# Grouped-query layer: mask addition and segment maximum in one VectorE instruction per 128 columns

## The reference

```python
scores = jnp.einsum('bkgld,bksd->bkgls', q, k) * scale
scores = scores + encoder_attention_mask[:, :, None, :, :]
attn = jax.nn.softmax(scores, axis=-1)
out = jnp.einsum('bkgls,bksd->bkgld', attn, v)
out = out.transpose(0, 3, 1, 2, 4).reshape(b, l, H)
out = out @ Wo + bo
x = out + hidden_state
mu = jnp.mean(x, axis=-1, keepdims=True)
var = jnp.var(x, axis=-1, keepdims=True)
return (x - mu) * jax.lax.rsqrt(var + EPS) * gamma + beta
```

## Time and profile before

| | |
|---|---|
| median of 3 runs | 2688.79 us (2685.13 to 2689.0) |
| profiled execution, its time | 2687.89 us |
| its span, first to last instruction | 2686.1 us |
| busy in the span: PE | 2477.0 us (92%) |
| DVE, ACT, POOL | 1280.0 (48%), 1089.2 (41%), 1106.1 us (41%) |
| layer 1 stands at | about 805 to 1190 us of the span |

### The profile page before, as it was taken

How to read it: one execution, slowest core, us unless ns; L and a number is a source line. 1 busy time by engine, 2 the same in 40 slices (tenths; PEclk the granted TensorE clock), 3 DMA queues, 4 the chain that set the end, 5 groups by cost and what they waited for, 6 DMA issues and landing times.

```text
span 2686.1 us, 47930 instructions
## 1 busy us (share of the span) xinstructions
PE 2477.0 (92%) x18464; PEld 2080.4 (77%) x18464; DVE 1280.0 (48%) x2527; ACT 1089.2 (41%) x3705; POOL 1106.1 (41%) x1972
## 2 busy tenths in 40 slices
PE   7999998999997788758889899999899999899999
PEld 5887886888886666647778788888788888688887
DVE  4555564323226878764555533322355555432322
ACT  4555553111117777754565511111355555311111
POOL 2454446400035888873454571003335444640000
PEclk9999999999998989878999999999999999999999
DMA  4112213111122222221232241102211211311100
GB/s 154 56 56 74 86 48 95 59 47 48 57 71 72 82 91 70 74 67 45 94 111 77 82 129 48 47 23 69 87 48 49 84 53 48 95 59 48 47 32 16
DMA packets 110320, 181.25 MB, mean 67 GB/s; under 512 B 7888, under 2 KB 43408, under 8 KB 109072
## 3 DMA queue, kind: packets, MB, share of 16 engines
q1 hardware_dynamic: 110096, 178.19, 20.2%
HBM read 132.02 MB, written 46.14 MB: 66 GB/s over the span
## 4 chain that ended last, share of the span: by engine, by line
PE 79%; DVE 8%; ACT 6%; POOL 3%; issue 3%; DMA 1%; SPq 0%; DVEq 0%; POOLq 0%; ACTq 0%
PE banks L317 70%; PE banks L453 4%; ACT plain_high L697 4%; PE banks L480 3%; DVE neg_max L948 2%; DVE plain_high L944 2%; POOL plain_high L1268 1%; DVE plain_work L953 1%; PE banks L504 1%; DVE rounded_work L1046 1%; DVE rounded_work L1020 1%; DVE stats L1072 1%; POOL rounded_high L308 0%; PE banks L442 0%; ACT plain_high L684 0%
## 5 line engine op out<-in xcount | busy, mean ns | idle before, releaser
L317 PE MATMUL banks<-rounded_work,rounded_low 128*128 128x512 f32 (+1 forms) x2688 | 534.7, 357 | 58.4 <-issue 35.2
L1268 POOL TENSOR_SCALAR plain_high<-plain_high,inv_sum 128x128 f32<-128x128 f32 (+1 forms) x1024 | 389.6, 403 | 410.2 <-DVE inv_sum L966 409.7
L317 PEld LDWEIGHTS banks<-rounded_work,rounded_low 128*128 128x128 f32 x2688 | 446.7, 200 | 125.6 <-issue 53.7
L317 PE MATMUL banks<-rounded_work,rounded_high 128*128 128x512 f32 (+1 forms) x2400 | 485.4, 356 | 8.4 <-DMA rounded_work<-ctx_split 5.8
L925 ACT ACTIVATE plain_work<-banks,columns 128x512 f32<-128x512 f32 x192 | 132.5, 690 | 865.3 <-PE banks L317 865.3
L317 PEld LDWEIGHTS banks<-rounded_work,rounded_high 128*128 128x128 f32 x2400 | 397.1, 191 | 75.8 <-issue 10.0
L1244 DVE CAST rounded_work<-plain_work 128x512 fp32r<-128x512 f32 x192 | 99.3, 517 | 694.1 <-ACT plain_work L925 682.9
L317 PE MATMUL banks<-rounded_low,rounded_work 128*128 128x512 f32 x1728 | 413.1, 391 | 0.0
L317 PE MATMUL banks<-rounded_high,rounded_work 128*128 128x512 f32 (+1 forms) x1728 | 392.7, 380 | 0.0
L317 PEld LDWEIGHTS banks<-rounded_low,rounded_work 128*128 128x128 f32 x1728 | 322.3, 188 | 68.8 <-issue 3.0
L317 PEld LDWEIGHTS banks<-rounded_high,rounded_work 128*128 128x128 f32 x1728 | 311.8, 190 | 60.4 <-issue 1.4
(11 more groups left out here) (101 smaller groups left out, 3055.3 us busy)
## 6 DMA issues: line engine op xcount, KB each, us to landing
plain_work<-x SPq DMA_DIRECT2D x96, 256.0 KB, 2.8
plain_work<-mlp_w SPq DMA_DIRECT2D x96, 256.0 KB, 2.7
rounded_work<-ctx_split SPq DMA_DIRECT2D x24, 1024.0 KB, 5.9
u<-plain_work SPq DMA_DIRECT2D x48, 256.0 KB, 3.1
plain_work<-u SPq DMA_DIRECT2D x12, 1024.0 KB, 7.2
x<-plain_work SPq DMA_DIRECT2D x48, 256.0 KB, 2.1
plain_work<-attention_w SPq DMA_DIRECT2D x44, 256.0 KB, 2.7
plain_work<-inputs_t SPq DMA_DIRECT2D x8, 1024.0 KB, 8.0
```

What stands on the lines that cost most here:

```text
L317: mm = pe.matmul(dst, lhs(i), rhs(j), start=first and n == 0, stop=last and n == 2, skip_group_check=True)
L1268: last = pool.tensor_scalar(part, part, inv_sum[:, R % 2, r, g:g + 1], 1.0, ALU.mult, ALU.mult)
```

## The change

The two VectorE instructions of a bank give way to four of a fused kind, one for each segment. `tensor_tensor_reduce` with these operands writes out = (score + mask) * -1 and gives accum = min(3e38, all of out), which is the negated maximum. The SBUF copy therefore holds negated masked scores, and ScalarE's exp takes scale -1 in this layer. The wait between the addition and the reduction, on VectorE itself, goes. `s_free[r]` is now counted after the last of the four instead of after the addition, `maxed` isn't counted in this layer, and ScalarE waits for `s_free[r]` in its place; the later layers' counts of `maxed` are moved accordingly.

```diff
         def act_exp(act, y, p, k, r):
             R = y.round(p, k)
             pr = prob(y)[R % 2]
-            act.wait_ge(maxed, 4 * R + r + 1)
+            if y.kind == GQA:
+                act.wait_ge(s_free[r], y.use(p, k) + 1)
+            else:
+                act.wait_ge(maxed, 4 * (R if y.n == 0 else R - L[1].rounds) + r + 1)
             for g in range(y.segs):
                 part = slice(g * y.seg, (g + 1) * y.seg)
-                src = pr[:, r, part] if y.kind == GQA else PS[:, r, part]
-                last = act.activation(pr[:, r, part], src, ACT.Exp, bias=neg_max[:, R % 2, r, g:g + 1],
+                gqa = y.kind == GQA
+                last = act.activation(pr[:, r, part], pr[:, r, part] if gqa else PS[:, r, part], ACT.Exp, scale=-1.0 if gqa else 1.0,
+                                      bias=neg_max[:, R % 2, r, g:g + 1],
                                       accum_out=row_sum[:, R % 2, r, g:g + 1])
             last.then_inc(exped if y.kind == GQA else s_free[r], 1)
...
                 b = of_round(y, k)[0]
                 if k == 0 and r == 0:
                     dve.wait_ge(qk_loaded[p % 2], 16 * (p // 2 + 1))
-                dve.tensor_tensor(pr[:, r, :].rearrange("p (u n) -> p u n", u=4), src.rearrange("p (u n) -> p u n", u=4),
-                                  qk_mask[:, p % 2, b, :].unsqueeze(1).broadcast_to([P, 4, P]), ALU.add).then_inc(s_free[r], 1)
-                dve.wait_ge(s_free[r], u + 1)
-                src = pr[:, r, :]
+                for g in range(4):
+                    part = slice(g * P, (g + 1) * P)
+                    last = dve.tensor_tensor_reduce(pr[:, r, part], src[:, part], qk_mask[:, p % 2, b, :], -1.0, 3.0e38, ALU.add, ALU.min,
+                                                    accum_out=neg_max[:, R % 2, r, g:g + 1])
+                last.then_inc(s_free[r], 1)
+                return
             dve.tensor_reduce(neg_max[:, R % 2, r, 0:y.segs], src.rearrange("p (g n) -> p g n", g=y.segs), AX.X, ALU.max,
                               negate=True).then_inc(maxed, 1)
```

## The result

The changed kernel takes 2673.35 us in the median of 4 runs (2672.15 to 2673.65), the kernel before 2688.89 us (4 runs, 2685.13 to 2691.57): the ratio is 0.994, with a 95% interval of 0.9928 to 0.9952. It is 15.5 us or 0.6% faster. The forecast was 2678 us, with a range that began at 2673: the direction and the place are as foretold, the size is half as large again, and the median lies 0.35 us inside the lower end.

The account below looks back on a forecast made before the run. Layer 1 was taken as bound by hand-overs between four engines, mainly VectorE and ScalarE: 58 banks x 0.20 us = 11.6, less 1, leaves -10.5; 2687.9 - 10.5 + 0.9 = 2678 us, range 2673 to 2727.

Parts of the forecast that it names:

- the later release: TensorE may rewrite a bank some 0.4 us later; claimed to cost nothing, covered by 4.9 us, else 13 us in all.
- The fused instruction: Four per bank on VectorE in layer 1, each 0.28 us alone and taking the engine for 0.21 us.
- The dearer row, with a scalar column: Upper bound for the fused instruction: the nearest VectorE row of that width, 342 ns alone, taking the engine 0.26 us.
- the wash: Rival: fused instruction 0.26 us plus write 0.07, a bank 1.32 us as before, no change, 2689 us; chance 0.17.
- The accumulator write: One after each fused instruction on VectorE: 0.07 us of the engine, no hold, making a segment 0.28 us.
- Held reads: Rival: VectorE's accumulator writes and fused instructions never overlap, a bank 1.72 us, 37 us slower, 2726 us; chance 0.23.
- The banks on the chain: Layer 1 banks whose saving counts: 58 of 128, between 61 from chain shares and 56 from 7 a pair.
- The cut for the other branch: 1 us taken from the 11.6 us gain for rounds where GpSimd's normalisation, with 0.25 us of wait, ends last.
- the rival that takes the gain: GpSimd's normalisations, 311 us of 385 busy, end last in layer 1: only -5.5 us, 2683 us; chance 0.07.
- All other stretches as long as before: Sign in the profile: the layer 1 window shorter by 10 us, everything outside it unchanged.
- 1.1 us from a bank's first start to the next bank's: Sign in the changed kernel's profile: the length of a layer 1 bank on VectorE, against 1.32 us before.
- The inversions' wait for exp: Sign on VectorE in layer 1: the wait for ScalarE should stay at 1.6 us or grow.

Follow-up runs that it names:

- e2: The changed kernel with an unread maximum over 392 columns ahead of each bank's fused instructions, so a bank takes 1.32 us again; 2687.8 us, ratio 1.0003 to the kernel before.
- e9: The changed kernel with an unread maximum over 280 columns ahead of each bank's fused instructions, bank 1.19 us; 2680.66 us, ratio 0.9978 to the kernel before.
- e3: The kernel before with its addition and reduction, but each bank released and handed to ScalarE by one count after the reduction; 2687.09 us, ratio 1.0001.
- e4: The changed kernel with bank 0 of each layer 1 round normalised on VectorE instead of GpSimd; 2664.45 us, ratio 0.9915 to the kernel before.
- e8: The kernel before with bank 0 of each layer 1 round normalised on VectorE instead of GpSimd; 2688.27 us, ratio 1.0005.

## Why the prediction was right and wrong

- **Place, sign, mechanism.** Right in these: the gain is the shorter bank on VectorE (e2, e9), in layer 1, and nothing came of the dropped wait, of ScalarE's constant, or of the later release (e3).
- **The fused instruction.** Right: 0.28 us alone and 0.21 us to the next start, from the addition's row and the row with constant scalars. The dearer row, with a scalar column, would have been wrong; so the wash falls.
- **The accumulator write.** Wrong: "I take 0.07 us and no hold". It has no hold, but it takes nothing at all of the engine. This made a bank 1.12 us instead of 0.84, and the saving of a bank 0.20 instead of 0.48. It is the step of the prediction that failed: the term was taken from one-column instructions that stand alone and from ScalarE's read the earlier trace rows, and neither behaves like this write. Held reads, the case for slower, are refuted by the same rows: the write starts 0.08 us before its fused instruction ends (908.79, and 908.59 + 0.284).
- **The banks on the chain.** Too few: "I use 58", from a pattern of 7 a pair. The slope between 1.32 and 1.07 us is (385.8 - 370.4) / 0.25 = 62 banks by the stretches and 71 by the ratios (17.7 us), against the 61 that the shares of the chain had given and the 64 of the chain by GpSimd. Rounding the measured share down to the pattern cost 7% or more.
- **The cut for the other branch.** Wrong in size: "I take 1 us". At the bank of 0.84 us the slope would give 0.48 x 62 = 30 us. The layer 1 stretch gave 19.9 and the kernel 15.5. GpSimd's list, which now waits once a pair, was named as the rival that takes the gain, with 0.25 us of slack read rightly; but it was priced against the small saving and given 0.07. Its "311 us of 385" is all of GpSimd's work; the normalisations alone are 181.6. In truth both hold: the larger saving ran into it. That it is the limit is shown by its timeline and by e4, and e8 agrees. Of the 10 us that layer 1 lacks against the slope, e4 gets 4.3 back before ScalarE's exps stand in its place.
- **The other layers.** "All other stretches as long as before" failed: behind layer 1 the changed kernel is 6.3 us longer (1493.3 against 1487.0) in the profiled executions. No term of the sum stood for it, and its cause is open.
- So errors went against each other: a saving more than twice as large, and a limit and longer later layers that together took half of it. That 15.5 us came out so near to the forecast's 10.5 is luck. Had the saving been the 0.20 us of the forecast, the slope by the stretches says 12.4 us and not 10.5.
- **The signs that were named.** "1.1 us from a bank's first start to the next bank's" failed, and pointed at the pair's price. The inversions' wait for exp did grow, from 1.6 us in each of 32 waits to 2.4 in each of 37. VectorE's share in the chain fell, but ScalarE's didn't rise (22.3% to 20.5%): GpSimd's did.

## What to carry to other kernels

Where four engines are each busy for three quarters of a stage, the chain names only the longest of several near-equal ones: before pricing a saving, follow the list of the busiest other engine from one wait to the next through a whole pair, and add up its idle times. Two of its waits alone (0.18 and 0.25 us here) make the limit look far too near; all four were 5.02 us a pair, and the gain of layer 1 used 2.37 of them. A fused operation with an accumulator was worth it at a width of only 128 columns, because it took away a second pass over the same data; four short instructions at 0.21 us beat two long ones at 0.72 and 0.60. When a saving stops short, unload the engine that took over into the wait that the saving has opened: here the wait between the two inversions took over a quarter of the normalisations, and the kernel became 7 to 9 us faster still, 4.3 of them in this layer.

## What the runs showed of the hardware

- VectorE's accumulator write (`DVE_READ_ACCUMULATOR2_ANT`, 82 ns) starts with the next instruction at the same time (908.79 and 908.79) and adds nothing to the start-to-start time of 0.21 us. ScalarE's accumulator read isn't free: after it the next activation starts 0.09 us later than the read, so it takes 0.09 us of that engine.
- The fused custom instruction over 128 columns is 284 ns alone, 5 ns above what the plain addition's rows extrapolate to (681 - 384 x 1.0475 = 279). It pays next to nothing for being fused.
- The extra reduction over 166, 280 and 392 columns was 323, 441 and 558 ns alone: 1.04 ns a column and 0.15 us fixed.
